# Expert outputs made beside a sort instead of beside a gather loop

## The reference, cut to what matters

```
h = (x_flat @ W_gat).reshape(M, HEADS, NUM_EXPERTS)
e = leaky_relu(a_src[src] + a_dst[dst])          # 524,288 random edges, and one loop a token
alpha = segment_softmax(e, dst)
agg = segment_sum(h[src] * alpha, dst)
scores = layernorm(agg).reshape(M, HEADS, NUM_EXPERTS).mean(1)
w = softmax(top 2 of the 4 scores)
out = x + sum over experts of g[e] * (gelu(x @ W1[e] + b1[e]) @ W2[e] + b2[e])
```

## Time and profile before

| what | value |
| --- | --- |
| median of three runs | 8344.9 us (8342.73 to 8347.91) |
| profiled execution, its own time | 8360.4 us |
| its span | 8358.7 us |
| busy PE, DVE, ACT, POOL | 3248.3, 3825.6, 2006.1, 4891.5 us |
| mean granted TensorE clock | 0.713 of full speed |
| DMA | 464.52 MB, 56 GB/s |

### The profile page before, as it was taken

The page is one execution under the profiler, slowest core; times in us unless marked ns, Lnnn a source line. Parts: engine busy times, 40 slices in busy tenths (PEclk is TensorE's granted clock), DMA queues, the critical chain, the costliest instruction groups (busy, mean ns, idle before and its releaser), DMA issues. The chain is left out here.

```text
span 8358.7 us, 49988 instructions
## 1 busy us (share of the span) xinstructions
PE 3248.3 (39%) x10147; PEld 1491.7 (18%) x10147; DVE 3825.6 (46%) x7442; ACT 2006.1 (24%) x3788; POOL 4891.5 (59%) x4842
## 2 busy tenths in 40 slices
PE   0011005888644443434434344343443444410134
PEld 0011003556411111111111111111111111100001
DVE  9998997888653222222222212222122221221488
ACT  0000004777522222222222222222222222210011
POOL 0000002555477777777777777777777777777552
PEclk9955557888777777767777677777777777765555
DMA  0000002344312121221212212122121221211266
GB/s 20 0 0 0 1 21 64 120 124 124 102 38 45 44 52 38 51 51 38 51 38 51 51 38 51 38 51 51 38 51 38 51 51 38 48 34 17 78 205 219
DMA packets 333987, 464.52 MB, mean 56 GB/s; under 512 B 158255, under 2 KB 233986, under 8 KB 317058
## 3 DMA queue, kind: packets, MB, share of 16 engines
q1 hardware_dynamic: 186282, 406.11, 14.0%
q0 software_dynamic: 147552, 56.95, 7.3%
HBM read 232.79 MB, written 229.93 MB: 55 GB/s over the span
## 5 line engine op out<-in xcount | busy, mean ns | idle before, releaser
L868 POOL DMA_INDIRECT e_got<-rows,e_index x4352 | 4128.3, 949 | 1327.1 <-issue 1327.1
L938 DVE TENSOR_TENSOR e_adv<-e_got,e_near 128x256 f32<-128x256 f32 x68 | 53.7, 789 | 3157.8 <-DMA e_got<-rows,e_index 3157.7
L1397 ACT ACTIVATE ex_hh<-ex_hid_ps,ex_b 128x512 f32<-128x512 f32 x1024 | 697.2, 687 | 1825.4 <-PE ex_hid_ps L1317 1824.6
L1358 PE MATMUL ex_out_ps<-ex_turned,ex_b 36*128 36x512 bf16 x64 | 38.5, 601 | 2634.4 <-DVE ex_o L1410 2634.4
L1416 DVE TENSOR_TENSOR ex_hs<-ex_hh,ex_gate_ps 128x512 f32<-128x512 f32 x512 | 346.1, 686 | 715.5 <-ACT ex_hh L1397 711.6
L1368 PE MATMUL ex_kept_ps<-ex_hh,ex_w 128*128 128x512 f32 x1024 | 548.4, 617 | 273.2 <-ACT ex_kept L1389 273.2
L1363 PE MATMUL ex_out_ps<-ex_hs,ex_w 128*128 128x512 f32 x1024 | 637.0, 707 | 0.6 <-DVE ex_hs L1416 0.6
L710 POOL MEMSET q_word<- 128x128 int16 x1 | 0.2, 205 | 1077.7 <-POOLq L89 1077.7
L1317 PE MATMUL ex_hid_ps<-ex_tn,ex_w 128*128 128x512 f32 x1024 | 577.3, 648 | 0.0
L1317 PE MATMUL ex_hid_ps<-ex_lower,ex_w 128*128 128x512 f32 x1024 | 522.9, 592 | 0.0
L1358 PEld LDWEIGHTS ex_out_ps<-ex_turned,ex_b 36*128 36x128 bf16 x64 | 6.5, 101 | 2686.4 <-DVE ex_o L1410 2686.4
(11 more groups left out here) (381 smaller groups left out, 6352.8 us busy)
## 6 DMA issues: line engine op xcount, KB each, us to landing
e_got<-rows,e_index POOLq DMA_INDIRECT x4352
kept<-ex_kept SPq DMA_DIRECT2D x64, 1024.0 KB
c_kept<-kept SPq DMA_DIRECT2D x64, 1024.0 KB, 5.7
sums<-e_out SPq DMA_DIRECT2D x68, 768.0 KB, 3.7
m_xin<-in_x_dram SPq DMA_DIRECT2D x64, 512.0 KB, 4.4
mid<-m_xm SPq DMA_DIRECT2D x64, 512.0 KB, 2.9
norm<-m_tn SPq DMA_DIRECT2D x64, 512.0 KB, 4.6
ex_tn<-norm SPq DMA_DIRECT2D x64, 256.0 KB, 4.8
```

The costliest lines, as they stand in the source:

```text
L868: pool.indirect_dma_start(got[:, at % 2, c, :], None, rows_d, bass.IndirectOffsetOnAxis(ap=index[:, at % 2, c:c+1], axis=0)).then_inc(S["g ...
L1397: act.activation(self.hh[:, s % 2, :], self.hid_ps[:, s % 2, :], ACT.Gelu, bias=self.b1[:, s % self.GATED // HID, s % HID:s % HID + 1]).th ...
```

## The change

The mixer comes first. The products of all 128 tiles, of both halves, are made in the block of the sort's network by a new class `Outputs`. It has two buffers for hidden values and two for outputs (`y_ps`), and stores each tile to `kept`. The key words of edges and tokens are both made in a first block ahead of the network; the products' weights (`Weights`) are loaded there too. PE, ACT and DVE get their orders from Python generators: the sort is cut into 429 units, the outputs into 129 rounds of 8 gaps, and `Pace` gives out 429/1032 of a unit at each gap, on every engine alike. A unit is one minimum or maximum on DVE; on PE and ACT it is empty, except for the four pairs of chunks of each crossing. The PSUM tile of the transposes is a ring of 4 cells of 512 columns; each crossing has 8 chunks.

In the gather loop the class `Upper` takes the place of `Experts`. Its gates are turned by PE (8 transposes in all) and stored in DRAM (`gate`). From round 4 on, SP loads for each tile of the upper half the gates, spread to all partitions (1 MB), `mid` (256 KB) and the kept outputs (1 MB); ACT copies the outputs to PSUM, DVE multiplies by the gates and adds. `finish_lower` and `gather_tokens` stay, and so does all of the attention.

Order of the blocks, in `program`:

```diff
-        sorter(nc, edges, keys[0], 0, flag[:, :])
+        mixer(nc, io, dict(xmid=mid, norm=norm, rows=rows.rearrange("(b j p) r -> b p j r", j=H*W//P, p=P), agg=agg[:, :, :], ROW=ROW))
+        weights = Weights(nc, ctx, io)
+        with ExitStack() as c0:
+            sort_keys(nc, edges, keys[0], 0, flag[:, :], Outputs(nc, c0, weights, norm, kept, 2 * TOKEN_TILES))
         low = Places(nc, ctx, 0)
         places(nc, keys[0], 0, low)
-        mixer(nc, io, dict(xmid=mid, norm=norm, rows=rows.rearrange("(b j p) r -> b p j r", j=H*W//P, p=P), agg=agg[:, :, :], ROW=ROW))
```

The outputs and the pace:

```diff
+class Outputs:
+    STEPS, GAPS, AHEAD = EXPERTS * HID, EXPERTS * HID, 3
+    def __init__(self, nc, ctx, weights, norm_d, kept_d, tiles):
+        def ps(n, shape): return ctx.enter_context(nc.psum_tensor(f"o_{n}", shape, F32))
+        self.nc, self.weights, self.norm_d, self.kept_d, self.TILES = nc, weights, norm_d, kept_d, tiles
+        self.ROUNDS = tiles + 1
+        self.S = ctx.enter_context(semaphores(nc, "o", "w ld0 ld1 ld2 ld3 hid gel y kept st0 st1"))
+        self.hid_ps = ps("hid_ps", [P, 2, TOK]); self.y_ps = ps("y_ps", [P, 2, TOK])
...
+    def buffers(self, ctx):
+        def sb(n, shape): return ctx.enter_context(self.nc.sbuf_tensor(f"o_{n}", shape, F32))
+        self.tn = sb("tn", [P, 4, TOK]); self.hh = sb("hh", [P, 2, TOK]); self.kept = sb("kept", [P, 2, EXPERTS, TOK])
+    def load(self, sp, r):
+        sp.dma_start(self.tn[:, r % 4, :], self.norm_d[r // 2, :, (r % 2) * TOK:(r % 2 + 1) * TOK]).then_inc(self.S["ld%d" % (r % 4)], 16)
...
+    def vector(self, v, r, u):
+        for _ in range(self.GAPS):
+            u()
+    def hidden(self, pe, g):
+        r, s = g // self.STEPS, g % self.STEPS
+        if s == 0:
+            pe.wait_ge(self.S["ld%d" % (r % 4)], 16 * (r // 4 + 1))
+        e, f = s // HID, s % HID
+        pe.matmul(self.hid_ps[:, g % 2, :], self.weights.w1[:, e, f*P:(f+1)*P], self.tn[:, r % 4, :], start=True, stop=True).then_inc(self.S["hid"], 1)
+    def tensor(self, pe, r, u):
+        S, last = self.S, self.STEPS * self.TILES
+        if r == 0:
+            self.hidden(pe, 0)
+            self.hidden(pe, 1)
+        for s in range(self.STEPS):
+            g = self.STEPS * r + s
+            if g < last:
+                e, f = s // HID, s % HID
+                pe.wait_ge(S["gel"], g + 1)
+                if f == 0:
+                    need(pe, S["kept"], EXPERTS * r + e - 1)
+                pe.matmul(self.y_ps[:, e % 2, :], self.weights.w2[:, e, f, :], self.hh[:, g % 2, :], start=(f == 0), stop=(f == HID - 1)).then_inc(S["y"], 1)
+                if g + 2 < last:
+                    self.hidden(pe, g + 2)
+            u()
+    def keep(self, act, n):
+        r, e = n // EXPERTS, n % EXPERTS
+        act.wait_ge(self.S["y"], HID * (n + 1))
+        if e == 0:
+            need(act, self.S["st%d" % (r % 2)], 16 * (r // 2))
+        act.activation(self.kept[:, r % 2, e, :], self.y_ps[:, e % 2, :], ACT.Identity, bias=self.weights.b2[:, e:e+1]).then_inc(self.S["kept"], 1)
+    def scalar(self, act, r, u):
+        S, last = self.S, self.STEPS * self.TILES
+        for s in range(self.STEPS):
+            g = self.STEPS * r + s
+            if g < last:
+                act.wait_ge(S["hid"], g + 1)
+                need(act, S["y"], g - 1)
+                act.activation(self.hh[:, g % 2, :], self.hid_ps[:, g % 2, :], ACT.Gelu,
+                               bias=self.weights.b1[:, s // HID, s % HID:s % HID + 1]).then_inc(S["gel"], 1)
+            if s % HID == 1 and HID <= g <= last + 1:
+                self.keep(act, g // HID - 1)
+            u()
+class Pace:
+    def __init__(self, parts, units, gaps):
+        self.parts, self.units, self.gaps, self.passed, self.given = parts, units, gaps, 0, 0
+    def __call__(self):
+        self.passed += 1
+        while self.given < self.passed * self.units // self.gaps:
+            next(self.parts, None)
+            self.given += 1
```

The network's parts that touch them, in `sort_keys`:

```diff
+    PAIRS, CELL, RING = 4, 512, 4
+    CHUNK = 2 * PAIRS
...
+        UNITS = COL_BITS * (COL_BITS + 1) + PART_BITS * (1 + 2 * (PAIRS + 1) + PART_BITS - 1 + 2 * (COL_BITS - 1))
...
+            def cross(a, b):
...
                 crossing_source.append(a)
+                settle()
                 v.sem_inc(to_turn, 1)
...
+                for pair in range(PAIRS):
+                    for c in (2 * pair, 2 * pair + 1):
+                        lo, _ = turned_of(x, c)
+                        olo, ohi = target_of(b, x, c)
+                        hi = copy_of(x, c)
+                        v.wait_ge(copied, CHUNK * x + c + 1)
+                        go(v.tensor_tensor(olo, lo, hi, ALU.min))
+                        go(v.tensor_tensor(ohi, lo, hi, ALU.max))
+                        used[x, c] = count[0]
+                    yield
...
+            if other:
+                pace = Pace(sorting_on, UNITS, other.ROUNDS * other.GAPS)
+                for r in range(other.ROUNDS):
+                    other.vector(v, r, pace)
...
+            def copy(x, c):
+                act.wait_ge(turned, CHUNK * x + c + 1)
+                _, hi = turned_of(x, c)
+                act.activation(copy_of(x, c), hi, ACT.Copy).then_inc(copied, 1)
...
+            def turn(x, c):
+                if c == 0:
+                    pe.wait_ge(to_turn, x + 1)
+                before = used.get((x, c - RING) if c >= RING else (x - 1, CHUNK - RING + c))
+                if before:
+                    pe.wait_ge(done, before)
                 source = crossing_source[x]
...
+                for i, g in enumerate(blocks_of(x, c)):
+                    last = pe.transpose(turned_ps[:, c % RING, i*P:(i+1)*P], source[:, g*P:(g+1)*P], ident[:, :])
+                last.then_inc(turned, 1)
+            def turning():
+                for now in merges():
+                    if now:
+                        x, pair = now
+                        for c in (2 * pair, 2 * pair + 1):
+                            turn(x, c)
+                    yield
```

The tile in the gather loop, in `Upper`:

```diff
+    def load(self, sp, at, turn):
...
+        sp.dma_start(self.gate[:, u, :, :].rearrange("p e t -> p (e t)"), self.gate_d[tile, :, :].broadcast_to([P, EXPERTS * TOK])).then_inc(S["ld%d" % u], 16)
+        sp.dma_start(self.xm[:, u, :], tile_of(self.mid_d, 1, at, turn, 4, 1 - self.FIRST)).then_inc(S["ld%d" % u], 16)
+        sp.dma_start(self.kept[:, u, :, :], self.kept_d[tile + TOKEN_TILES, :, :, :]).then_inc(S["ld%d" % u], 16)
...
+        act.wait_ge(S["ld%d" % (at % 2)], self.ready(at, turn))
+        for e in range(EXPERTS):
+            need(act, S["stt"], EXPERTS * (t - 1) + e + 1)
+            act.activation(self.y_ps[:, e, :], self.kept[:, at % 2, e, :], ACT.Copy).then_inc(S["cp"], 1)
...
+        for e in range(EXPERTS):
+            v.wait_ge(S["cp"], EXPERTS * t + e + 1)
             if e == 0:
...
+                v.tensor_tensor(self.acc_ps[:, :], self.y_ps[:, e, :], self.gate[:, u, e, :], ALU.mult).then_inc(S["stt"], 1)
+                continue
+            need(v, S["add"], (EXPERTS - 1) * t + e - 2)
+            v.tensor_tensor(self.z[:, e % 2, :], self.y_ps[:, e, :], self.gate[:, u, e, :], ALU.mult).then_inc(S["stt"], 1)
+            v.wait_ge(S["stt"], EXPERTS * t + e + 1)
+            need(v, S["add"], (EXPERTS - 1) * t + e - 1)
+            v.tensor_tensor(self.acc_ps[:, :], self.acc_ps[:, :], self.z[:, e % 2, :], ALU.add).then_inc(S["add"], 1)
...
+        v.tensor_tensor(self.o[:, u, :], self.acc_ps[:, :], self.xm[:, u, :], ALU.add).then_inc(S["fin"], 1)
```

More of the change, by code:

```diff
@@ L447, in sorter, with crossing @@
+        def crossing(x):
+            for pair in range(PAIRS):
+                yield x, pair
+            yield None
+        crossing_source, used = [], {}
         final_low, final_high = [ping], [u_b]
+        if other: other.buffers(ctx)
+        block = ctx.enter_context(nc.Block())
         @block.sync
         def _(sp):
-            sp.dma_start(src[:, :], edge_rows[0]).then_inc(loaded, 16)
-            sp.dma_start(dst[:, :], edge_rows[1]).then_inc(loaded, 16)
-            sp.wait_ge(const, 1)
@@ L519, in _ @@
[L519 to L529, removed]
@@ L584, in _, with run @@
+            def run(part):
+                for _ in part:
+                    pass
+            final = []
+            sorting_on = sorting()
+            if other:
+                pace = Pace(sorting_on, UNITS, other.ROUNDS * other.GAPS)
+                for r in range(other.ROUNDS):
+                    other.vector(v, r, pace)
+            run(sorting_on)
+            a, b = final
+            settle()
             go(v.tensor_tensor(b[:, :], a[:, :], upper[:, :], ALU.min))
             go(v.tensor_tensor(upper[:, :], a[:, :], upper[:, :], ALU.max)); settle()
-            v.sem_inc(iota_free, 1)
+            v.sem_inc(spent, 1)
@@ L595, in _ @@
[L595 removed]
+                run(step(a, b, 1 << (s - 1)))
+                a, b = b, a
+            settle()
+            final_low[0] = a
+            v.sem_inc(spent, 1)
```

(28 more changed lines are left out.)

679 lines of the change are left out of this document (332 added, 347 removed).

## The result

Four runs of the changed kernel took 9301.4 us in the median (9299.3 to 9306.0), against 8345.3 us for four of the kernel before. The ratio is 1.1146, with a 95% interval of 1.1127 to 1.1166: 956 us slower. The forecast was 9302 us, +957.

What follows compares the result with a forecast made beforehand. POOL's gathers were taken to bound the gather loop and DVE the sort, with PE bounding the sort after the change. Stage terms summed to 9316 us, +957 over the profiled 8358.7; added to the median 8345, 9302 us, range 9210 to 9600.

Steps and rivals of the forecast that it cites:

- What leaves the gather loop: worth nothing: Gather loop: products, gelus and gating lie beside POOL's gathers at 1.25 us each, so removing them gains 0.
- 16 us that were kept for the low end: Gather loop: the most that freeing DVE could give back to POOL's gathers; taken as 0 in the forecast.
- The network's stage: Sort's network with the added products: PE becomes the bound, 5 + 1761 + 123 = 1889 us.
- 0.86 us a product: Sort's network: 2,048 fp32 products of 128x512 on PE at full clock, 1761 us in all.
- 2.2 us a pair: Network's crossings: transposes, two ACT copies, a gelu and hand-overs before PE's next product; 56 pairs, 123 us.
- What moves: Stages around the network: mixer, places and tail keep their times; second key words 33.9, iota 3.6, block end 4 us.
- The sum: Whole kernel: stage terms give 9316 us against 8358.7, +957; added to the median 8345, 9302 us.
- (a): Network's stage: dense products get 0.87 of full clock, 1761 becomes 2024 us, +263, 9565 us; chance 0.13.
- (b): Products beside the sort: a 1.43 us stall remains at every expert, +732, 10034 us; chance 0.05.
- (c): Gather loop: products' traffic or waits cause the gathers' pitch or issue; without 1327 us, 7975 us; chance 0.03.
- (e): Gather loop: new loads of 2.5 MB a tile hold the gathers up, +912, 10214 us; chance 0.03.
- (d): Network's stage: a product is one matmul record, 881 us under DVE's 930, so no cost, about 8350; chance 0.01.

Runs made afterwards that it cites:

- narrow products: Kernel before with every expert product of the gather loop 32 columns wide in place of 512: 8348.7 us, ratio 1.0000.
- bare loop: Changed kernel without the tiles' loads, copies, weighing and upper-half store beside the gathers: 9296.2 us, against 9300.8 for the changed kernel beside it.
- order alone: Kernel before with the mixer's stage put in front of the sort, nothing else: 8351.2 us, ratio 1.0004.
- copies later: Changed kernel with ScalarE copying a crossing's chunks one slot later, behind the next gelu: 9232.5 us.
- half-products run: Changed kernel with the products of 64 tiles beside the sort in place of 128, each output stored twice: 8477.5 us, ratio 1.0156 to the kernel before.

## Why the prediction was right, point by point

**The gather loop.** "What leaves the gather loop: worth nothing" held: 9 us in the spans, of which 6.5 are the execution of before and 2.6 can be the removed work, and none in the medians when the products are made narrow. The narrow products and the bare loop show that neither products nor loads nor copies set the 1.25 us. Of the 16 us that were kept for the low end, some 2.6 came, so the copies taken off DVE gave back next to nothing. A gather beside DVE's operation with two SBUF inputs still takes longer (1.07 us at 5007.51, for 1.10 in the earlier trace rows), as that operation stayed.

**The network's stage.** 1889 us forecast, 1885.8 measured (1045.5 to 2931.3). Its term of 0.86 us a product is in the steady rows of PE:

```profile
1054.29 1.02 PE L506 MATMUL o_y_ps<-o_hh,w_w 128*128 128x512 f32 x2
1055.15 1.02 PE L493 MATMUL o_hid_ps<-o_tn,w_w 128*128 128x512 f32 x2
1056.00 1.02 PE L506 MATMUL o_y_ps<-o_hh,w_w 128*128 128x512 f32 x2
```

The 2.2 us a pair, built from rows that showed no such copy, is 2.19, and that it fits to the digit is luck: the copy takes 0.38 us where 0.44 was taken, PE's next product comes after 2.09 us, and the other 0.10 is the product behind it, which starts 0.96 us later and not 0.86, a term that the sum didn't have. DVE stayed ahead: it stood 961 us at the 56 pairs waiting for ACT's copies, for 46 before, and PE never waited for it in the network.

**What moves.** The words, load, iota and block end are 94.4 us (951.1 to 1045.5) for a sum of 94.8. The tail is 107.2 for 107.8. The order alone was shown to cost nothing.

**The sum.** It was 17 us too long as a span: 9316 against 9298.6. Of these, 9 are the loop (5454.1 for 5445.0 between first and last gather), 7 the way to the first gather (3237.3 measured; 2935.2 + 107.8 + 189.3 + 12.3 = 3244.6 by the sum; 3 of the 7 are the network), and 1 the rest. The spans differ by 940 us and not 957. The medians differ by 956, since the profiled execution of before stood 15.5 us above its median and that of after 1 below. So the last digits of the forecast are luck: two differences of some 16 us met. 6.5 us of loop belong to both, as the profiled loop of before was that much longer than in the version with the mixer in front. The runs of the kernel before in this study reach from 8342.7 to 8356.5 us, and the profiled one took 8360.4, so a single execution of it can be off by that much; by the medians beside it the changed kernel is 952 to 956 us slower.

**The rivals.** (a) fell: the network's window is granted 1.00 in the mean, its first 5.6 us apart, although PE stands for 1.05 us at each of 56 pairs. The rule of the Trainium skill on micro-idles between PSUM groups ("TensorE: Matmul & The Clock Gate", section "A second HAM failure mode: psum-queue depth-cycling") let one expect that the clock could swing here; the trace does not agree for pauses of this length and rate. (b) fell: in the network PE waits for ACT at the 56 pairs alone, never at an expert, and with one buffer in this order 133 us came, not 732. (c) and (e) fell by the narrow products and the bare loop. (d) fell with the first row of products: two records each, 0.86 us apart.

**Where my model was wrong, outside the forecast:** the loop of before has a second limit of 54.45 us a chunk, which was hidden under 80 us of gathers, and which I put at 38 when first asked. In the prediction the 9286 us with POOL's 16 us given back is called the sum; it is the forecast of 9302 less 16.

None of the versions beats the kernel before. The best of the changed kernel, with the copies later, is 9232.5 us. The loop that it relieves waits for nothing but its gathers, and the products take 1761 us where the sort's network took 930, so a better order can't bring it under 8345. In the half-products run even 64 of 128 tiles beside the sort cost 1.6%.

## What to carry to other kernels

Work that is hidden behind a full engine is free where it stands; before moving it, ask what the stage that it leaves waits for (here, POOL's idle time was all issue) and how much room the stage that it enters has on that engine (here 930 us, 83 of them in use, for 1884). Find the second limit of the relieved stage as well: it says from which point the move pays, here from half of the gathers down (0.997 at half). When work is woven into another's order, the price is at the seams, and the order of three instructions on one engine (copy, gelu, kept copy) was worth 68 us.

## What the runs showed of the hardware

- An indirect gather of 128 rows costs POOL 0.947 us and 0.30 us of issue in this loop (0.949 in the profiled execution of before), whether PE is 40% busy (mixer in front), 22% (narrow products) or idle, and whether 51 or 20 GB/s pass in all (changed kernel, bare loop). With 16 gathers a chunk in the changed kernel, and DVE 90% busy, it took 0.965.
- TensorE keeps 1.00 of its clock (2.4 GHz) over 1.88 ms of fp32 products with 56 stops of 1.05 us. Their first 5.6 us (1048.4 to 1054.0) were granted 0.57, after 72 us in which PE had nothing to do.
- Narrowing a product from 512 to 32 columns left 56% of PE's busy time in the loop (1220 of 2172 us), as the granted clock fell to 0.50 there and a product of 32 columns with its weight load still shows as records of some 0.4 us.
